# The first pair of heads woven with the feed-forward's end, and layer norms with two tensor operands

## The reference

```python
def _layernorm(x, axis=-1, eps=1e-05):
    m = jnp.mean(x, axis=axis, keepdims=True)
    v = jnp.var(x, axis=axis, keepdims=True)
    return (x - m) / jnp.sqrt(v + eps)
...
    x = x + 0.5 * _L0_ffn_ref(_layernorm(x, axis=-1), L0_ffn_w_gate_up, L0_ffn_w_proj)
    x = x + _L0_attn_ref(_layernorm(x, axis=-1), L0_attn_w_qkv, L0_attn_w_out)
    x = x + 0.5 * _L0_ffn_ref(_layernorm(x, axis=-1), L0_ffn_w_gate_up, L0_ffn_w_proj)
    x = x + 0.5 * _L1_ffn_ref(_layernorm(x, axis=-1), L1_ffn_gate_w, ...)
    x = x + _L1_attn_ref(_layernorm(x, axis=-1), L1_attn_W_Q, L1_attn_W_K, L1_attn_W_V)
    x = x + 0.5 * _L1_ffn_ref(_layernorm(x, axis=-1), L1_ffn_gate_w, ...)
```

```python
        q = _apply_rope(q, cos, sin)
        k = _apply_rope(k, cos, sin)
        scale = 1.0 / math.sqrt(D)
        logits = jnp.einsum('bqhd,bkhd->bhqk', q, k) * scale
        attn = jax.nn.softmax(logits.astype(jnp.float32), axis=-1).astype(logits.dtype)
        out = jnp.einsum('bhqk,bkhd->bqhd', attn, v)
```

## Time and profile before

| | us |
|---|---|
| median of 3 executions | 1762.16 |
| lowest, highest | 1758.46, 1764.87 |
| the profiled execution | 1760.51 |
| its span in the profile | 1758.7 |
| PE busy | 1645.4 (94%) |
| DVE busy | 1287.1 (73%) |
| ACT busy | 1219.9 (69%) |
| POOL busy | 1126.1 (64%) |

### The profile page before, as it was taken

One profiled execution on the slowest core, in us unless ns is written; L12 is line 12 of the kernel. 1 busy time (PEld: TensorE's weight loads), 2 busy tenths in 40 slices (PEclk: granted clock), 3 DMA queues, 4 the chain that ended last, 5 costly groups with the idle time before them and its releaser, 6 DMA issues.

```text
span 1758.7 us, 26693 instructions
## 1 busy us (share of the span) xinstructions
PE 1645.4 (94%) x9307; PEld 963.8 (55%) x9307; DVE 1287.1 (73%) x2427; ACT 1219.9 (69%) x1886; POOL 1126.1 (64%) x747
## 2 busy tenths in 40 slices
PE   0898789999999999999999999998999999899998
PEld 0565345555555555555555555554565565676565
DVE  7877657777777777767777777786687778886766
ACT  6655778888888888988988888874654443325432
POOL 0554768888888888888888878883763222653222
PEclk9999899999999999999999999999999999999999
DMA  8100567887888878889878788784001210000001
GB/s 284 49 1 19 101 115 144 139 138 144 150 150 146 147 140 154 148 135 164 144 136 152 130 145 151 128 137 89 0 1 58 64 40 1 1 1 28 28 10 48
DMA packets 580506, 174.03 MB, mean 99 GB/s; under 512 B 543243, under 2 KB 579350, under 8 KB 580246
## 3 DMA queue, kind: packets, MB, share of 16 engines
q1 hardware_dynamic: 580374, 172.33, 51.8%
HBM read 35.94 MB, written 2.10 MB: 22 GB/s over the span
## 4 chain that ended last, share of the span: by engine, by line
PE 73%; DVE 8%; POOL 2%; issue 2%; ACT 1%; SPq 0%; DMA 0%; DVEq 0%; POOLq 0%; ACTq 0%
PE banks L1789 23%; PE banks L1790 23%; PE banks L1791 23%; DVE X L1644 1%; POOL sq_sum L684 1%; DVE mo_h L1631 1%; DVE nmax L1463 1%; DVE x L1196 1%; PE banks L1887 1%; PE banks L1855 1%; PE banks L1888 1%; PE banks L1856 1%; PE banks L1939 0%; PE banks L1799 0%; PE banks L2100 0%
## 5 line engine op out<-in xcount | busy, mean ns | idle before, releaser
L737 POOL TENSOR_TENSOR Pl<-Pm,Ph 128x1024 f16<-128x1024 f32 x256 | 546.4, 2134 | 52.3 <-ACT Ph L962 51.3
L952 ACT ACTIVATE Pm<-banks,nbias,s_scale 128x1024 f32<-128x1024 f32 x256 | 308.0, 1203 | 135.9 <-DVE nbias L1465 135.7
L1463 DVE TENSOR_REDUCE nmax<-banks 128x1 f32<-128x1024 f32 x256 | 312.6, 1221 | 111.6 <-PE banks L1791 110.5
L962 ACT ACTIVATE Ph<-Pm 128x1024 f16<-128x1024 f32 x256 | 268.3, 1048 | 1.2
L716 POOL TENSOR_TENSOR rp_b<-rp_s,rope 128x512 f32<-128x512 f32 x128 | 162.8, 1272 | 150.9 <-ACT rp_s L929 150.9
L1502 DVE SCALAR_TENSOR_TENSOR X<-banks,rinv,X 128x256 f32<-128x256 f32 x256 | 112.7, 479 | 156.8 <-PE banks L1791 156.8
L790 POOL TENSOR_TENSOR mT_lo<-mo_h,mT_hi 128x512 f16<-128x512 f32 x72 | 83.7, 1162 | 214.2 <-ACT mT_hi L1064 213.9
L1789 PE MATMUL banks<-QK_hi 128*128 128x512 f16 x512 | 197.1, 385 | 6.8 <-DVE QK_lo L1539 2.7
L1789 PE MATMUL banks<-PT_hi,V_hi 128*128 128x512 f16 x512 | 194.9, 381 | 3.2 <-DMA PT_lo<-Pl 3.2
L1790 PE MATMUL banks<-QK_lo,QK_hi 128*128 128x512 f16 x512 | 195.5, 382 | 0.0
L1791 PE MATMUL banks<-QK_hi,QK_lo 128*128 128x512 f16 x512 | 195.5, 382 | 0.0
(11 more groups left out here) (240 smaller groups left out, 4136.4 us busy)
## 6 DMA issues: line engine op xcount, KB each, us to landing
moe_raw<-in_L_ffn_W SPq DMA_DIRECT2D x72, 128.0 KB, 2.3
w_all<-in_L_attn_w_qkv SPq DMA_DIRECT2D x3, 2048.0 KB, 16.5
a_raw<-in_L_attn_w_qkv SPq DMA_DIRECT2D x24, 256.0 KB, 3.1
PT_hi<-Ph SPq DMA_TRANSPOSE x256, 3.4
PT_lo<-Pl SPq DMA_TRANSPOSE x256, 3.4
raw_gu<-in_L_ffn_w_gate_up SPq DMA_DIRECT2D x2, 1024.0 KB, 7.3
X<-in_L_attn_x SPq DMA_DIRECT2D x2, 1024.0 KB, 13.1
o_raw<-in_L_attn_w_out SPq DMA_DIRECT2D x8, 256.0 KB, 3.4
```

Source lines behind the costliest of these rows:

```text
L737: nc.gpsimd.tensor_tensor(Pl[:, z % 4, :], Pm[:, k, :], Ph[:, z % 4, :], ALU.subtract).then_inc(pl_done.sem, 1)
L952: nc.scalar.activation(Pm[:, k, :], two_banks[z % 2][:], ACT.Exp, bias=nbias[:, z:z + 1], scale=s_scale[:], accum_out=rsum[:, z:z + 1]).th ...
L962: nc.scalar.activation(Ph[:, z % 4, :], Pm[:, (base * SLOTS + z) % 3, :], copy).then_inc(ph_done.sem, 1)
L1463: nc.vector.tensor_reduce(nmax[:, z:z + 1], two_banks[z % 2][:], AX, ALU.max, negate=True).then_inc(max_done.sem, 1)
```

## The change

Three things change.

**The end of the first feed-forward and the start of the first pair run interleaved.** On PE the last four down projections no longer stand in one row ahead of the projections: one stands before the first, the squares behind the second, one between the third and fourth projection, and two around the values. VectorE's additions and lower parts and ScalarE's copies follow the same order. The values go to banks 1 and 2, the last down projections to banks 7 and 6, and SBUF is laid out again so that the tiles of both stages don't overlap where both live; `rp_q` moves with that.

**In the first pair** ScalarE writes `QK_hi` ahead of the slot's exponential (it stood behind the exponential and the side work). `QK_lo` of projections 3 to 7, which GpSimd wrote, is written by VectorE. The two `ln_variance`, fourteen small instructions, move from ahead of the first maximum to behind the maxima of slots 0 and 1, and the eight normalisations of the slots from four and four in slots 1 and 4 to two each in slots 1 to 4. GpSimd's two `rsqrt_ln` move into slots 1 and 2.

**Every layer norm** normalises with `scalar_tensor_tensor` in place of `tensor_scalar`: the mean is still a scalar for each row, and the reciprocal root is read as a second tensor of 128 x 256 with a step of zero.

```diff
@@ layer norms, VectorE @@
                 for t in (half * TPH + j for j in tiles):
-                    nc.vector.tensor_scalar(XN[:, t, :], X[:, b, t, :], mean[:, b, t:t + 1], rstd[:, b, t:t + 1],
-                                            ALU.subtract, ALU.mult).then_inc(xn_ready.sem, 1)
+                    nc.vector.scalar_tensor_tensor(XN[:, t, :], X[:, b, t, :], mean[:, b, t:t + 1], rstd[:, b, t:t + 1].broadcast_to([P, D]),
+                                                   ALU.subtract, ALU.mult).then_inc(xn_ready.sem, 1)
...
@@ the first pair's slots, VectorE @@
                     if has_slots(body):
                         maximum(s)
+                    if body == "first" and s == 0:
+                        first_rope_lo(3)
+                    if body == "first" and s >= 2:
+                        for side in SIDES["first"][s - 2]:
+                            if side.name == "qk" and side.d == 0:
+                                first_rope_lo(side.i)
...
-                    if body == "first" and s in (1, 4):
-                        ln_normalise(1, 1, (1, 4).index(s))
+                    if body == "first" and s < NHALF:
+                        ln_variance(1, 1, s)
+                    if body == "first" and 1 <= s <= 4:
+                        ln_normalise(1, 1, (s - 1) // 2, range((s - 1) % 2 * 2, (s - 1) % 2 * 2 + 2))
...
+            def first_rope_lo(j):
+                k = (PRE_QKO if j < 4 else QKO)[j % 4]
+                part = (slice(None), j // 4, k // 2, slice(k % 2 * HALF, (k % 2 + 1) * HALF))
+                dve.wait_ge(qk_hi.sem, qk_hi.in_pair(0, j + 1))
+                nc.vector.tensor_tensor(QK_lo[part], rp_q[:, j % 2, :], QK_hi[part], ALU.subtract).then_inc(qk_lo.sem, 1)
...
@@ the first pair's slots, ScalarE @@
+                    if body == "first":
+                        if s == 0:
+                            rope_hi(3, of(rope_sum, 4))
+                        for side in sides_of(s - 2):
+                            rope_hi(side.i, of(rope_sum, side.i + 1, side.d))
                     if has_slots(body):
                         exponentials(s)
                     for side in SIDES[body][s]:
                         side_work(side)
                     if has_slots(body):
-                        if s == 0 and body == "first":
-                            rope_hi(3, of(rope_sum, 4))
-                        for side in sides_of(s - 2):
-                            rope_hi(side.i, of(rope_sum, side.i + 1, side.d))
+                        if body != "first":
+                            for side in sides_of(s - 2):
+                                rope_hi(side.i, of(rope_sum, side.i + 1, side.d))
                         probs_hi(s)
...
@@ the first pair's slots, GpSimd @@
+                    if body == "first" and s in (1, 2):
+                        rsqrt_ln(1, 1, s - 1)
                     if s:
                         probs_lo(s - 1, 0)
                     elif has_before(body):
                         probs_lo(SLOTS - 1, -1)
                     if has_slots(body):
-                        if s == 0 and body == "first":
-                            rope_lo(3, of)
                         for side in sides_of(s - 3):
+                            if body == "first" and side.d == 0:
+                                continue
                             rope_lo(side.i, lambda sig, i, d=side.d: of(sig, i, d))
...
@@ PE, ahead of the first pair @@
-                x_ready(0, 1, 0)
+                last_down(0)
                 pe.wait_ge(w_lo_done.sem, w_lo_done.in_head(0, 1))
                 project(0, 0, bank[3], PRE_QKO)
                 pe.wait_ge(w_lo_done.sem, w_lo_done.in_head(0, 2))
                 project(0, 1, bank[0], PRE_QKO)
-                pe.wait_ge(x_added.sem, x_added.before(0, 1))
+                last_squares()
+                pe.wait_ge(x_added.sem, x_added.before(0, 1) - TPH)
+                project(0, 2, bank[4], PRE_QKO)
+                last_down(1)
+                project(0, 3, bank[5], PRE_QKO)
                 pe.wait_ge(w_lo_done.sem, w_lo_done.in_head(0, 3))
-                values(0, 0, bank[7])
-                values(0, 1, bank[6])
-                x_ready(0, 1, 1)
-                project(0, 2, bank[4], PRE_QKO)
-                project(0, 3, bank[5], PRE_QKO)
+                values(0, 0, bank[1])
+                last_down(2)
+                values(0, 1, bank[2])
+                last_down(3)
...
@@ VectorE, ahead of the first pair @@
                 dve.wait_ge(rope_in.sem, 16)
                 rope_cos(0, bank[3], pre(rope_shift, 2), PRE_QKO)
+                last_down(0)
+                rope_add(0, bank[3], pre)
                 rope_cos(1, bank[0], pre(rope_shift, 4), PRE_QKO)
-                rope_add(0, bank[3], pre)
                 rope_add(1, bank[0], pre)
-                values_lo(0, 0, bank[7], pre(v_hi_done, 1))
...
-                for half in range(NHALF):
-                    ln_variance(1, 1, half)
+                values_lo(0, 1, bank[2], pre(v_hi_done, 2))
+                for j in (2, 3):
+                    last_down(j)
                 attention_pair("first", 0)
```

More of the change, by code:

```diff
@@ L187, in build_program @@
     ff_h = sb("ff_h", [P, 3, HALF], f32)
+    hT_at = place["at"]
     hT_hi = sb("hT_hi", [P, NHALF, FT, HALF], f32r)
@@ L263, in build_program @@
     Pm = sb("Pm", [P, 3, S], f32)
+    rp_q = sb("rp_q", [P, 2, HALF], f32)
     rp_s = sb("rp_s", [P, 2, HALF], f32)
@@ L774, in attention @@
                     rope_sine(j, pre, PRE_QKO)
-                for half in range(NHALF):
-                    rsqrt_ln(1, 1, half)
                 attention_pair("first", 0)
@@ L1424, in ffn @@
                     add(len(PHASES) - 1, j)
-                    if f and j == 1:
+                    if j == 1:
                         expert_weights_lo(1)
@@ L1773, in _ @@
                 ln_statistics(0, 0, t)
-            ffn(0, 0)
-            attention()
+            attention(ffn(0, 0))
             ffn(1, 2)
@@ L1864, in squares @@
                     for j in range(TPH):
-                        last = nc.tensor.matmul(bank[5][:, D + j:D + j + 1], sq_sum[:, phase % NHALF, (FT - 1) % 2, j * P:(j + 1) * P], ones,
+                        last = nc.tensor.matmul(bank[END_SQUARES[f] if phase == len(PHASES) - 1 else 5][:, D + j:D + j + 1], sq_sum[:, phase % NHALF, (FT - 1) % 2, j * P:(j + 1) * P], ones,
                                                 start=True, stop=True)
```

91 lines of the change are left out of this document (48 added, 43 removed).

## The result

The changed kernel ran in 1766.24 us (median of 18, 1763.81 to 1773.41) against 1762.25 us for the kernel before (18 runs, 1758.46 to 1764.87). The ratio of the runs is 1.003, 95% interval 1.0021 to 1.0039: slower by 0.2 to 0.4%. That is 4.0 us by the medians and 5.3 us by the ratio; the forecast was 1767 us, +5.0. The profiled execution took 1766.07 us, its span 1764.3 us, 5.6 us over the span before.

A forecast was written before the change was run, and what follows sets the result against it. PE was taken to set the end, with gains only at its gaps between feed-forward and attention. -4.5 + 0 + 1.5 + 8.0 = +5.0 us on 1760.5, plus 1.65 to the run median, gave 1767 us; range 1753 to 1779.

The forecast's parts named there:

- part 1: Feed-forward to first maximum: interleaving removes two PE waits, 3.3 us, and moved variance saves 1.5 us; taken as -4.5 us.
- part 2: First pair's slots: shorter normalisation blocks against VectorE instructions caught behind GpSimd's Pl; taken as 0 us.
- part 4: Every layer norm: two-tensor normalisation adds 0.29 us per unblocked four and still waits for GpSimd; +8.0 us.
- part 3: First pair's slots: more small gaps leave PE's clock low longer; -3 to +3 us, taken as +1.5.
- the upper end, 4.8: Up to the first maximum: largest gain, 3.3 us of PE waits plus 1.5 us of ln_variance instructions.
- the ends of -3.8 and +4.2: First pair's slots: normalisations without waits save 3.8 us; two instructions caught behind a Pl cost 4.2 us.
- upper end of +13: Layer norms: all 24 fours at +0.29 us, 7.0, plus retention's waits and both ends of the pairs.
- the form escapes the lock: Layer norms: two-tensor normalisation no longer waits for GpSimd; 1754.5 us, down to 1750; chance 0.10.
- Half rate: Layer norms: two-tensor normalisation takes two cycles an element, 0.27 us more each; 1789 us; chance 0.04.
- Rival 3: Layer norms: normalisations no dearer than before, 0 instead of 8.0 us; 1759 us; chance 0.04.
- rival 4: First pair: lower parts and ln_variance each caught behind a Pl, maximum late in two slots; +4.2, 1771 us; chance 0.13.
- Rival 1: First pair: QK_lo leaving GpSimd and the broken 5.22 us block gain 3.8 us, no clock term; 1762 us; chance 0.19.

The follow-up runs named there:

- e1: Changed kernel with the one-tensor normalisation (tensor_scalar) of before everywhere, interleaving and slots kept: 1757.55 us, ratio 0.9969 to the kernel before.
- e10: Kernel before with the first-pair slots of e7 and the one-tensor normalisation, without the interleaving (weave): 1758.29 us, ratio 0.9972 to the kernel before.
- e7: Changed kernel with the one-tensor normalisation and the first pair's five QK_lo back on GpSimd: 1751.35 us, ratio 0.9948 to the kernel before.
- e3: Changed kernel with the one-tensor normalisation and the first pair's slots as before, only the interleaving (weave) left: 1757.83 us, ratio 0.9975 to the kernel before.
- e12: e7 with the first pair's QK_hi back behind the exponential and side work: 1754.43 us, ratio 0.9961 to the kernel before.
- e2: Kernel before with only the two-tensor normalisation (scalar_tensor_tensor) in every layer norm: 1774.47 us, ratio 1.0070 to the kernel before.
- e8: Changed kernel with GpSimd writing zeros instead of the probabilities' lower part in slots 0 to 4 of the first pair: 1763.02 us, ratio 1.0005 to before.
- e4: Changed kernel with the two-tensor normalisation only in the first feed-forward, one-tensor elsewhere: 1757.01 us, ratio 0.9972 to the kernel before.
- e5: Changed kernel with the two-tensor normalisation only in the last pair's slot 9, one-tensor elsewhere: 1756.43 us, ratio 0.9970 to the kernel before.

## Why the prediction was right

The sum hit, 1767 against 1766.24 us, and its mechanisms mostly too. That it hit to within 1 us is luck: part 1 came out 1.5 us better than forecast, part 2 1.1 us worse and part 4 0.7 to 2.7 us dearer, and the low clock of part 3 came with the form, in other places than forecast.

**Part 1**, weave and variance, -4.5. Measured to the first maximum -6.0 us without the form (e1), -5.6 with it. The maximum did not come near 165.5 us, as the forecast had it, but at 169.03, since the first feed-forward ended 4.7 us late. The weave is 4.0 (e10 to e7) to 4.7 us (e3), the variance 1.3 (e1 against e3) to 2.0 (e10). So the upper end, 4.8, was too low. It counted PE's recorded waits and the busy time of the fourteen instructions, and the traces show what it left out. Before, the scores of the first slot were done at 167.37 us and the maximum began at 169.94, 2.57 us late, behind the fourteen instructions and, ahead of these, the cosine product and sum of the fourth projection:

```profile
166.99 0.38 PE L1791 MATMUL banks<-QK_hi,QK_lo 128*128 128x512 f16 x1
```

```profile
167.79 0.69 DVE L1451 TENSOR_TENSOR rp_q<-banks,rp_b 128x512 f32<-128x512 f32 x1
```

In e1 VectorE waits for the scores, and the maximum follows 0.04 us behind them:

```profile
164.37 1.23 DVE L1483 TENSOR_REDUCE nmax<-banks 128x1 f32<-128x1024 f32 x1 [0.16 <-PE banks L1812]
```

So of the 6.0 us, 2.5 are VectorE's lateness, where part 1 had the variance's 1.5, and the scores themselves come 3.5 us earlier behind the sixth four, near its 3.3.

**Part 2**, the slots, 0. Measured +1.7 us to the ninth maximum in the changed kernel, of which 0.6 is the form's and stands in part 4, so +1.1 (e1), inside the ends of -3.8 and +4.2. The 0 was a mean over edits that work against each other: the lower parts on VectorE cost 2.1 us (e7) and the upper parts ahead of the exponential win 2.1 us (e12). The waits came where they were priced, behind `Pl`: 2.01, 1.80 and 3.49 us.

**Part 3**, the clock, +1.5. The mean granted clock of all runs was 0.9897 after and 0.9903 before (the 27 runs beside e1), 1.1 us of the span. But the place was wrong, and the size is luck: the first slots show 0.80 from 170 to 196 us, a higher clock than the 0.74 before, and the low clock came in the first feed-forward and in retention. It goes with the form rather than with the slots: without the form the mean was 0.9915 (e1), and with the form alone 0.9868 (e2).

**Part 4**, the form, +8.0. Measured 8.7 us by the medians and 10.7 by the ratios (e1). The rule by which it was priced holds: 0.29 us for each unblocked four (1.67 us at 24.37, 1.38 before), and still a wait for GpSimd, shown by e8. Its places, measured in profiles with like clock: first feed-forward 1.1 us, 0.5 to the first maximum, and second feed-forward 1.5 (forecast for both 3.2); first pair 0.6 to the ninth maximum (0.7); last pair 2.2 (2.1); retention 1.8, in e8, which had no low stretch there (2.0). The experts, priced at 0, took 0.7 us. Together 8.4. The 2.3 us up to the 10.7 are likely low clock, since e1's mean of 0.9915 against 0.9897 is up to 3 us. What the single places are worth in the whole time was within the noise of e4 and e5. So their sum is shown, by e1, and its split only by the timelines of single profiles. The forecast's upper end of +13 is more than its own terms give: 7.0 + 2.0 + 2.1 + 0.7 = 11.8.

The rivals: that the form escapes the lock is refuted by single normalisations of up to 2.36 us and by e8. Half rate is refuted too: unblocked ones take 0.466 us, and four in a row 1.67 us. (The rule of the Trainium skill, "Vector Engine (DVE) Microarchitecture Reference", section 7 ("Points that are easy to get wrong"), that a scalar_tensor_tensor with two SBUF sources that aren't bf16 runs at half throughput, the trace doesn't bear out for this form, one of whose tensors is a broadcast.) Rival 3, a form that costs nothing, is out by e1. Of rival 4 the mechanism came true, lower parts and variance caught behind a `Pl` with the maximum queued behind them, but at +1.1 us of its +4.2, nearer the 0 taken. Rival 1 was wrong: PE's waits in the first slots fell only from 13.7 to 12.7 us, and taking `QK_lo` off GpSimd, its first reason, cost 2.1 us (e7).

## What to carry to other kernels

Moving work from GpSimd to VectorE, or to a form that reads a scalar as a second tensor, gained nothing here, since the new instruction reads two tensors from SBUF while GpSimd reads: price it by the longest GpSimd operation beside it, not by its own length. Look at what is queued behind it; a maximum that gates the next exponential pays for every wait ahead of it. And a package with a small result is worth taking apart: here the weave, the variance and the upper parts won some 8 us, and the form and the lower parts cost some 12. And where a result is late, count its whole lateness, from the moment when its inputs are ready: here 2.57 us, of which the forecast counted 1.5.

## What the hardware showed unexpectedly

A small instruction waits like a large one: a tensor_scalar of 128 x 4 stood 2.01 us until GpSimd's operation was over. GpSimd's memset of 128 x 1024 did not hold VectorE's subtraction of two SBUF tensors (0.68 us beside it), but it did hold such a small tensor_scalar (0.81 us in place of 0.17, both in e8). The granted clock falls in short stretches, most of them 3.4 us long, an estimated 1.7 us of PE's work each, in places that differ from one execution to the next. The runs of one kernel spread with it: the changed kernel from 1763.81 us at a mean clock of 0.993 to 1773.41 us at 0.984. So a single profile tells 2 us of a stretch only where the clock of that stretch is the same in both.
